# Mamba scan: carried states of even chunks copied by ScalarE, and an eighth product with B on GpSimd in even chunks

## What is computed

```
h_l[e,n] = exp(delta_l[e] * A[e,n]) * h_(l-1)[e,n] + delta_l[e] * x_l[e] * B_l[n]
y_l[e]   = sum over n of h_l[e,n] * C_l[n]
```

## Time and profile before

| | |
|---|---|
| median of 3 runs | 1921.82 us (1918.57 to 1923.24) |
| the profiled execution | 1917.6 us, span of its instructions 1915.9 us |
| the Mamba scan | about 41 to 903 us of the span |
| busy over the whole span | PE 92%, DVE 75%, ACT 57%, POOL 55% |
| busy in the Mamba scan, 372 to 905 us | DVE 519.7, POOL 509.1, PE 463.6, ACT 407.7 of 533.0 us |
| starts of chunks 3 to 7 (first scan) | 373.0, 479.2, 584.9, 691.1, 796.7 us |

### The profile page before, as it was taken

How to read it: one execution, slowest core, us unless ns; L and a number is a source line. 1 busy time by engine, 2 the same in 40 slices (tenths; PEclk the granted TensorE clock), 3 DMA queues, 4 the chain that set the end, 5 groups by cost and what they waited for, 6 DMA issues and landing times. The chain is left out here.

```text
span 1915.9 us, 26914 instructions
## 1 busy us (share of the span) xinstructions
PE 1756.1 (92%) x9643; PEld 1385.4 (72%) x9643; DVE 1435.7 (75%) x2217; ACT 1083.5 (57%) x1870; POOL 1061.3 (55%) x633
## 2 busy tenths in 40 slices
PE   6888989898998989767999999999999899999999
PEld 2556666665656666656788888888888688888888
DVE  4799999999999999999766656664444755555565
ACT  6777786878787876777344333342333443333433
POOL 3889999999999999999511111111445411111011
PEclk9898999999999999889999999999999999999999
DMA  6223332333333332261000000000000000000000
GB/s 195 85 80 106 100 100 94 95 105 92 105 92 102 104 101 92 79 208 50 1 1 1 0 0 1 1 22 6 1 0 1 1 11 11 11 11 11 11 12 12
DMA packets 59091, 101.11 MB, mean 53 GB/s; under 512 B 11120, under 2 KB 11248, under 8 KB 58864
## 3 DMA queue, kind: packets, MB, share of 16 engines
q1 hardware_dynamic: 58992, 99.88, 16.6%
HBM read 95.14 MB, written 4.72 MB: 52 GB/s over the span
## 5 line engine op out<-in xcount | busy, mean ns | idle before, releaser
L383 POOL TENSOR_TENSOR m_U<-m_U,m_C 128x1024 f32<-128x1024 f32 x255 | 600.8, 2369 | 25.7 <-DVE m_U L890 15.5
L525 PEld LDWEIGHTS m_y<-ident,m_U 128*128 128x128 f32 x2048 | 252.4, 148 | 118.1 <-issue 70.9
L890 DVE TENSOR_TENSOR_SCAN m_U<-m_dA,m_carry,m_U 128x512 f32<-128x512 f32 x256 | 311.4, 1272 | 5.2 <-ACT m_dA L758 4.8
L525 PE MATMUL m_y<-ident,m_U 128*128 128x128 f32 x2048 | 284.7, 285 | 30.4 <-POOL m_U L383 30.3
L890 DVE TENSOR_TENSOR_SCAN m_U<-m_dA,m_U 128x512 f32<-128x512 f32 x256 | 296.5, 1209 | 11.5 <-ACT m_dA L758 8.2
L758 ACT ACTIVATE m_dA<-high,m_negA 128x512 f32<-128x512 f32 x256 | 172.4, 685 | 71.5 <-DVE m_U L890 71.0
L758 ACT ACTIVATE m_dA<-even,m_negA 128x512 f32<-128x512 f32 x256 | 170.7, 684 | 54.1 <-DVE m_U L890 53.0
L1102 POOL TENSOR_TENSOR SW<-g_Rt 128x1024 f32<-128x1024 f32 x16 | 31.6, 1997 | 258.3 <-ACT g_Rt L1287 258.3
L1282 ACT ACTIVATE g_sil<-g_psG 128x512 f32<-128x512 f32 x96 | 57.6, 600 | 156.1 <-PE g_psG L1161 155.9
L1282 ACT ACTIVATE f_sil<-f_psG 128x512 f32<-128x512 f32 x96 | 57.5, 599 | 151.3 <-PE f_psG L1161 150.8
L1102 POOL TENSOR_TENSOR SW<-f_Rt 128x1024 f32<-128x1024 f32 x16 | 31.6, 1997 | 190.6 <-ACT f_Rt L1287 190.6
(11 more groups left out here) (369 smaller groups left out, 4383.2 us busy)
## 6 DMA issues: line engine op xcount, KB each, us to landing
m_C<-bc_rows SPq DMA_DIRECT2D x256, 256.0 KB, 3.2
m_B<-bc_rows SPq DMA_DIRECT2D x60, 256.0 KB, 3.6
even<-in_ffn_w SPq DMA_DIRECT2D x16, 256.0 KB, 4.9
out<-res SPq DMA_DIRECT2D x8, 512.0 KB, 2.8
res<-in_x SPq DMA_DIRECT2D x1, 3072.0 KB, 13.4
res<-in_x SPq DMA_DIRECT2D x2, 512.0 KB, 4.3
turned<-in_Wkvqu SPq DMA_DIRECT2D x1, 1024.0 KB, 4.8
high<-in_in_w SPq DMA_DIRECT2D x1, 512.0 KB, 4.6
```

What stands on the lines that cost most here:

```text
L383: pool.tensor_tensor(u, u, C[:, M % C_RING, :].unsqueeze(1).to_broadcast([P, PE_E, CHUNK]), ALU.mult).then_inc(hc_ready, 1)
L525: last = nc.tensor.matmul(y[:, t, j * P:(j + 1) * P], U[:, M % U_RING, j, t * P:(t + 1) * P], ident[:, :], start=False, stop=n == N - 1, i ...
L890: nc.vector.tensor_tensor_scan(u, dA[:, s % A_RING, :], u, carry[:, e, n:n + 1] if q else 0.0, ALU.mult, ALU.add).then_inc(scan_done, 1)
```

## The change

The carried states of even chunks are copied by ACT, in a new `keep_carry(M - 1)` between the two decays of iteration M, and no longer by POOL; POOL's C product still waits on `carry_ready` for the copy of its unit. In even chunks `ON_POOL` becomes the same as in odd ones: in half 0 the B product of unit 11 is made by POOL in place of unit 10's, and in half 1 those of units 19, 22, 26 and 30 (within the half 3, 6, 10, 14) in place of 20, 25 and 30 (4, 9, 14), one more than before.

```diff
-    ON_POOL, AHEAD = ((3, 7, 10, 14), (4, 9, 14), (3, 7, 11, 14), (3, 6, 10, 14)), 3
+    ON_POOL, AHEAD = ((3, 7, 11, 14), (3, 6, 10, 14), (3, 7, 11, 14), (3, 6, 10, 14)), 3
@@ gpsimd
                 pool.wait_ge(scan_done, PE_E * (M + 1))
                 if q == 0:
-                    pool.tensor_copy(carry[:, pair(p), n], u[:, :, CHUNK - 1]).then_inc(carry_ready, 1)
                     pool.wait_ge(carry_ready, UNITS * (c // 2) + N * p + n + 1)
@@ scalar
+            def keep_carry(M):
+                c, q, p, n = place(M)
+                if q == 0:
+                    act.wait_ge(scan_done, PE_E * (M + 1))
+                    nc.scalar.activation(carry[:, pair(p), n], U[:, M % U_RING, :, CHUNK - 1],
+                                         ACT.Copy).then_inc(carry_ready, 1)
+
             for M in range(ALL_UNITS):
                 if 0 < M < ALL_UNITS - 1:
                     decay(PE_E * (M + 1))
+                    if M > 0:
+                        keep_carry(M - 1)
                     decay(PE_E * (M + 1) + 1)
```

## The result

The changed kernel takes 1934.2 us (median of 4 runs, 1933.46 to 1934.57) against 1921.5 us of the kernel before: a ratio of 1.0073, with a 95% interval of 1.0060 to 1.0086. The two medians differ by 12.7 us, where 8.4 was forecast (by the ratio it is 14.0 us); the range of 1921 to 1940 us holds it.

What follows compares the result with a forecast made beforehand. DVE, POOL and PE were taken as near their limit, with POOL setting the pace from unit 19 after the change. Four even chunks at 2.1 us gave +8.4 us on the 1921.8 us median: 1930.2 us, range 1921 to 1940.

Steps and rivals of the forecast that it cites:

- The mechanism: Even chunks: POOL's C product now waits for ACT's copy, queued behind ACT's parts and a decay; 2.1 us a chunk.
- rival (c): Late C products delay PE's sums, projections, ACT's parts and the next C product: 3.9 us a chunk, 1937.5 us; chance 0.15.
- The price of a copy on ACT: 32 copies per even chunk, about 0.20 us long, next operation 0.10 us later: at most 6.4 us of 23 us free.
- Half 0: Up to gate0: DVE waits 0.9 us more at unit 7, units 11 and 14 near even; gate0 taken as unshifted.
- Units 19 to 30: POOL sets the pace without a gap from unit 19's C product; unit 30's scans start 2.65 us later.
- The end of the chunk: DVE's 0.54 us wait for PE goes, so the next chunk starts 2.1 us later instead of 2.65.
- Chunk 0: One of four even chunks, each counted alike at +2.1 us.
- What the profile was to show: POOL waits some 2 us at units 2, 13, 19; DVE waits at 7, 22, 30; chunk 107 to 108 us.
- (a): POOL's relief counts if ACT is at most some 2 us behind: 3.5 us a chunk saved, 1907.9 us; chance 0.12.
- (b): Half 0's late start is absorbed and gate0 comes 1.1 us early: 1.0 us lost a chunk, 1925.8 us; chance 0.18.

Runs made afterwards that it cites:

- the run with the copies alone: Kernel before with only the copies moved to ACT and its old lists kept (seven B products on POOL in even chunks): ratio 1.0093 to the kernel before, 17.5 us slower.

## Why the prediction was right, and where it was short

The mechanism was right where the forecast had put it, at units 7, 19 and 30; the size was short. By the number alone it need not have been this mechanism: 1934.2 us lies 4.0 us over the forecast and 3.3 us under the 1937.5 of rival (c). What tells them apart is the trace. Chunk 4 of the kernel after, on a scale that starts with the chunk's first scan:

| | forecast | measured |
|---|---|---|
| DVE at gate0 | 60.1 less 0.2, taken as unmoved | 60.6 |
| C product of unit 19 starts | 69.5 | 70.1 |
| unit 30's scans start | 100.9 | 102.1 |
| the next chunk starts | 107.7 | 109.3 |

**The price of a copy on ACT** was right, in duration (0.19 us) and pitch: 556.16 to 556.26, 0.10 us. The errata section of "VectorE: DVE Perf Modes" in the Trainium skill fits the duration; its latency between instructions doesn't show here behind a large one, where the next operation starts 0.10 us later, and the runs with and without copies agree with the row.

**Half 0** was the term that I sized too small. "In half 0 I count that and nothing more", 0.9 us at unit 7. Unit 7 cost 0.84 us, but units 11 and 14, which I had called close to even, cost 0.33 and 0.49 us. Counted from start to start of DVE's instructions, the three cost 1.9 us. Against them stand the product that DVE no longer makes, 1.1 us, and a wait at unit 15 that fell from 0.6 to 0.3 us. So DVE came to gate0 0.5 us later than before in place of 0.2 us earlier. ACT's slot 19 followed gate0 one to one, as forecast: its first decay started 68.58 us into the chunk before and 69.12 after. Of the forecast's shortfall in chunk 4, 3.6 - 2.1 = 1.5 us, this is 0.6.

**Units 19 to 30** were taken as gapless. POOL idled 0.33 us ahead of unit 23's C product (569.74), for ACT's copy again (569.41 to 569.60), and the steps were a little over 2.31 us; the stretch took 32.1 us from the C product of unit 19 to the scans of unit 30 for 31.4 forecast. That is another 0.6 us.

**The end of the chunk** gave back 0.24 us and not 0.54: DVE still waited 0.30 us for PE.

**Chunk 0** lost 4.5 us, 2.4 more than forecast and the largest part of the shortfall. I took it as any other, though in its half 0 ACT is far behind (DVE waited 5.7 us for its decays before), and its copies with it; half 0 grew from 63.9 to 65.7 us. I have no run on it alone.

**What the profile was to show.** POOL waited 1.9 us ahead of unit 2 and 1.8 us ahead of unit 19, as forecast, but only 1.2 us ahead of unit 13, and 1.3 us ahead of unit 1, which the forecast doesn't have. DVE waited for POOL's B products of units 7, 22 and 30, but also for those of 11, 14, 19 and 26. POOL was less busy by 2.4 us and not by 4: I had taken off the copies' full 0.19 us each, and their rows overlap with the C product before them. The chunk took 109.3 us, over the 107 to 108 forecast.

The rivals: (a) has its condition shown by the runs without the wait, which gave some 10 of its 14 us, but the condition fails in the change. (b), half 0 absorbed, is shut out by the trace. (c), a loop through PE that closes, doesn't show: PE waited longer for POOL's C products (6.8 us in chunk 4 for 3.8), but DVE's wait for PE fell from 1.5 to 0.3 us. But a shorter loop, past PE, which the prediction did not list, does close once. POOL's B product of unit 22 made DVE's scans wait 1.45 us. ACT then waited 0.96 us for the scans of unit 23 before a decay (565.84), as it did not at this place before, and so its copy of unit 23 came late enough to hold POOL up for the 0.33 us named above.

## What to carry to other kernels

A tiny operation moved to an engine with room takes its place in that engine's order with it. What it costs is not its 0.1 us but the wait for what stands in front of it in that queue, where someone's next work hangs on its result. Before moving, read from the trace when the new engine would get to it, unit by unit, against when its reader starts now. If some are late, put the operation ahead of the long parts, where the engine waits in any case: here that turned 12.7 us of loss into some 5 us of gain with the same instructions. And shares of busy time told nothing here: in the run with the copies alone both engines that had been full had slack in chunk 4, and it was no faster than the changed kernel.

## What the runs showed of the hardware that I had not expected

Nothing new in durations. One surprise is how exactly an odd chunk repeats: chunks 3 and 5 took 106.18 to 106.22 us in all fourteen kernels, whatever shift the even chunk before had left, so that a delay in an even chunk is passed on whole. The last chunk does not repeat like this, 106.1 to 109.4 us. The other surprise is how much of it goes with TensorE's granted clock although DVE is the fullest engine: the one wait for PE early in the last chunk grew from 1.20 us at a granted clock of 0.96 to 2.51 us at 0.71.
